# Second spline layer: eight slices in sixteen as rounded halves, and another order of the work between the two spline layers

## The chip, the cores and the metric

The kernel runs on one core of one Trainium2 chip. The metric is the device time of one execution in microseconds; lower is better. The profiled execution gives the trace that all rows are from.

## The reference, cut to what matters

A batch of 32 images and texts becomes 164 tokens each of width 192 (5248 rows in all), which pass attention and then a network of two spline layers with a residual. The change lies in the second of these layers.

```
def bspline_basis(x, num_cp=16, degree=3, rmin=-4.0, rmax=4.0):   # (N, D) -> (N, D, 16)
    ...
def kan_layer(x, w):                       # w: (Dout, Din, num_cp)
    return jnp.einsum('ndk,odk->no', bspline_basis(x), w)
...
# h: (5248, 192); w1: (512, 192, 16); w2: (192, 512, 16); n: the layer norm
y = h + kan_layer(kan_layer(layernorm(h), w1), w2)
```

So layer 2 is a product of 5248 rows with 512 x 16 = 8192 terms each by an 8192 x 192 matrix, all in float32.

## The kernel before

The program is written by hand: each engine has its queue of instructions in a fixed order, and semaphores tie them together. `wait_ge(s, n)` holds an engine's queue until s has reached n. The spline phase (`spline_phase`, from L1507) comes after attention and ends the kernel.

**Layer 1** works on 16 tiles (`PAIRS`) of 328 tokens. Per tile VectorE forms masks times basis values (`take1`, L1715) into a ring of four buffers `spline1_f`, and TensorE multiplies them in eight halves j by the weights, which are stored as a rounded high part and a rounded rest (`w_high`, `w_low`, three matmuls each, L1949 to L1951). TensorE counts a half as done on `f_used`. ScalarE empties the four sums of a tile into `hid` (`empty`, L1879), and SyncE stores them to `hid_scr` (`leave`, L1592, counted on `hid_out`).

**Layer 2** works on 41 tiles (`OT`) of 128 tokens. A tile q has four groups i = 0 to 3, a group sixteen slices r of 128 terms. The first `SETS` = 7 slices of a group go as rounded halves: the high half of the values against both halves of the weights in one matmul of 384 columns (L1977), and the low half of the values against the high half of the weights (192 columns, L1978). The other nine are full float32 matmuls (L1981), which the trace shows as two records each. Group 0 uses the values themselves (`v_high`, `v_low`, `b_`), groups 1 to 3 the values times a mask, which VectorE forms with three instructions each (`take2`, L1726: high, low, rest, of `SPLIT` = 896, 896 and 1152 elements). Before that the values of a tile need:

- on ScalarE `before2` (L1846): positions (four activations, L1842), three folds (L778, L780, L782), the outer square (L786); then `after2` (L1854): rounding to the interval number n (L775) and the inner square (L789, L791); and `high2` (L1864), the rounded high half of the values
- on VectorE `outer` (L799), `inner` (L803), `minus_value` (L1732), and `low2` (L1703), the low half
- at the end of a tile VectorE adds the residual from the sum (`leave`, L1794, L1797), and SyncE stores it.

`tile2` (L1765 on VectorE, L1917 on ScalarE) sets the order: VectorE prepares tile q + 1 between the masks of tile q.

**Between the layers** lies the change. The weights of layer 2 take the place of those of layer 1: raw weights are loaded into room that layer 1's halves leave (`RAW_FREE`, `REST_FREE`), ScalarE rounds them to the high half in four parts (`weight2_high(i)`, L1869, when `f_used` reaches `HIGH_FREE[i]`), and VectorE forms the low half (`weight2_low(i)`, L1762). TensorE waits in tile 0 ahead of each group for `w2_in[i]`, for `w2_ready` at i + 1, and for its masks. ScalarE's order between the layers, by hand:

```
high2(0, 0)
weight2_high(0)
weight2_high(1)
act.wait_ge(f_ready, L1F * PAIRS)
before2(0, 1, 1)
after2(1, 1)
weight2_high(2)
before2(1, 2, 0)
empty(PAIRS - 1)
weight2_high(3)
high2(1, 1)
```

`f_ready` at `L1F * PAIRS` says that VectorE has formed all of layer 1's masks. `share` (L103) lays several groups of buffers over the same room.

Of the kernel before, what the change touches and what calls it, by code (L numbers as in the profile page):

```python
# [19 lines left out]
F32 = mybir.dt.float32  # L20
F32R = mybir.dt.float32r
# [4 lines left out]
P = 128  # L26
# [17 lines left out]
PAIRS = B // 2  # L44
PT = 2 * TOK
# [1461 lines left out]
def spline_phase(nc, front, a, h_scr, hid_scr, step_scr, out, w_raw, w1_in):  # L1507
# [9 lines left out]
    MC = HID // P  # L1517
# [6 lines left out]
    C2_ = 4 * HID  # L1524
    SETS = 7
    SPLIT = SETS * P
# [3 lines left out]
    with ExitStack() as stack:  # L1530
        sb, ps, sem = memories(nc, stack)
        layer1_weights = [(f"spline1_weights_{k}", [P, HALVES, HALF * HID], F32R) for k in ("low", "high")]
        raw_weights = [("spline2_under", [P, HALVES * HALF * HID], F32), ("spline2_weights_raw", [P, 4, SETS * D], F32)]
        layer2_room = [(f"spline2_v_{k}{u}", [P, SPLIT], F32R) for k in ("high", "low") for u in range(2)] + [
            ("spline2_s", [P, C2_], F32), ("spline2_f_low1", [P, SPLIT], F32R),
            ("spline2_gap", [P, HIGH_AT - 5 * SPLIT - C2_], F32),
            ("spline2_weights_split", [P, 2, 4, SETS * D], F32R), ("spline2_weights", [P, 4, 4 * CH - SETS, D], F32)]
        (w_low, w_high), (_, w2_raw), spare = share(nc, stack, layer1_weights, raw_weights, layer2_room)
        v_high, v_low, s_ = [y[:] for y in spare[0:2]], [y[:] for y in spare[2:4]], spare[4][:]
        w2_split, w2 = spare[7:9]  # L1540
        f, f2 = share(nc, stack, [(f"spline1_f{i}", [P, C2_], F32R) for i in range(RING)],
                      [(f"spline2_f_high{i}", [P, SPLIT], F32R) if n == 0 else
                       (f"spline2_f{i}", [P, C2_ - SPLIT], F32) for i in range(1, 4) for n in range(2)] +
                      [(f"spline2_f_low{i}", [P, SPLIT], F32R) for i in range(2, 4)] +
                      [("spline2_f_gap", [P, C2_ - 2 * SPLIT], F32)])
        f_high, f_rest = (None, *f2[0:6:2]), (None, *f2[1:6:2])
        f_low = (None, spare[5], *f2[6:8])
        step_to, step_from = sb("spline2_step_to", [P, PART]), sb("spline2_step_from", [P, PART])
        n_, t_, a_, b_ = ([of, sb(f"spline_{k}1", [P, C2_])] for k, of in
                          (("n", front.n), ("t", front.t), ("a", front.a), ("b", front.b)))  # L1550
        bias2, x, xn = front.bias2, front.x, front.xn
        hid = [sb(f"spline1_hid{m}", [P, PT]) for m in range(MC)]
        acc = ps("spline1_acc", [P, MC, 512])
# [141 lines left out]
        def _(dve):  # L1695
# [69 lines left out]
            def tile2(tt, u, first=False, more=True, early=False):  # L1765

                q, v = 2 * tt + u, 1 - u
                if first:
                    weight2_low(0)
                    weight2_low(1)  # L1770
                take2(q, u, 1)
                if more:
                    front.outer(nc, dve, PAIRS + q + 1, a_[v][:], t_[v][:])
                if first:
                    weight2_low(2)
                take2(q, u, 2)
                if more:
                    front.inner(nc, dve, PAIRS + q + 1, b_[v][:], t_[v][:])
                    minus_value(q + 1, v)
                if first:  # L1780
                    weight2_low(3)
                take2(q, u, 3)
                if more:
                    low2(q + 1, v)
                if not first:
                    leave(tt - 1 if u == 0 else tt, q - 1, v, early)
# [31 lines left out]
        def _(act):  # L1818
# [85 lines left out]
            act.wait_ge(f_used, S_FREE)  # L1904
            high2(0, 0)
            weight2_high(0)
            weight2_high(1)
            act.wait_ge(f_ready, L1F * PAIRS)
            before2(0, 1, 1)
            after2(1, 1)  # L1910
            weight2_high(2)
            before2(1, 2, 0)
            empty(PAIRS - 1)
            weight2_high(3)
            high2(1, 1)
# [232 lines left out]
```

## Time and profile before

| | before |
|---|---|
| median of 3 runs | 2387.16 us (2383.34 to 2398.32) |
| the profiled execution | 2391.56 us, its span 2389.8 us |
| mean granted TensorE clock | 0.978 of 2.4 GHz |
| TensorE matmuls busy | 2277.9 us (95%) |
| VectorE busy | 1846.9 us (77%) |
| ScalarE busy | 1411.4 us (59%) |

The span runs from the first to the last instruction; the time of the execution lies 1.8 us above it. Layer 1 runs from about 857 to 1558.5 us of the span, layer 2 from there to 2386.9. All start times are microseconds from the start of the span. In the rows PE is TensorE's matmuls, PEld its weight loads, DVE VectorE, ACT ScalarE, POOL GpSimd.

### The profile page before, as it was taken

What the parts mean: (1) busy time and instruction counts of PE and PEld (TensorE: products, weight loads), DVE (VectorE), ACT (ScalarE), POOL (GpSimd) and SP (SyncE); (2) the same over time, 40 slices, a digit from 0 to 9 for tenths busy, and PEclk for the clock granted to TensorE, in tenths of its full rate; (3) what the DMA queues carried; (4) which work ended last, traced back from release to release, by engine and by line L of the source; (5) the groups of instructions that cost most, each with busy time, mean ns of one, the idle gap of its engine ahead of it and who ended that gap; (6) DMA issues with size and microseconds to landing.
All of it is one profiled execution on the core that took longest, in us unless ns stands there. A gap on an engine that the chain in (4) does not pass through costs nothing.

```text
span 2389.8 us, 49107 instructions
## 1 busy us (share of the span) xinstructions
PE 2277.9 (95%) x20033; PEld 2134.9 (89%) x20033; DVE 1846.9 (77%) x2241; ACT 1411.4 (59%) x1391; POOL 302.1 (13%) x169
## 2 busy tenths in 40 slices
PE   6599989999999989999999999979999999999999
PEld 5366777888888789999999999979999999999999
DVE  7699756666666587776767766579999999999995
ACT  6488303444444554435435345399888888888881
POOL 7622000000000021322322321000000000000000
PEclk9799998999999889999999999989999999999999
DMA  6655241111111101111111110210000000000000
GB/s 206 179 155 149 67 153 28 51 47 48 48 47 48 36 26 47 42 46 53 46 50 45 49 52 24 88 62 24 23 23 23 23 23 23 23 23 23 23 19 10
DMA packets 115454, 129.98 MB, mean 54 GB/s; under 512 B 17063, under 2 KB 106167, under 8 KB 115127
## 3 DMA queue, kind: packets, MB, share of 16 engines
q1 hardware_dynamic: 95215, 103.54, 14.5%
q10 hardware_dynamic: 16520, 14.34, 2.0%
q0 software_dynamic: 3616, 10.54, 1.7%
q8 instruction: 87, 1.43, 0.2%
q14 instruction: 16, 0.13, 0.0%
HBM read 92.79 MB, written 35.58 MB: 54 GB/s over the span
## 4 chain that ended last, share of the span: by engine, by line
PE 62%; ACT 1%; DVE 0%; issue 0%; ACTq 0%
PE spline_acc L1981 20%; PE spline_acc L1950 10%; PE spline_acc L1949 10%; PE spline_acc L1951 9%; PE spline_acc L1977 9%; PE spline_acc L1978 4%; PE spline_xT L764 0%; ACT spline_s L1842 0%; ACT spline_weights_split L1869 0%; DVE spline_f L1715 0%; ACT spline_t L778 0%; ACT spline_t L780 0%; ACT spline_front L778 0%; ACT spline_front L780 0%; ACT spline_t L782 0%
## 5 line engine op out<-in xcount | busy, mean ns | idle before, releaser
L1950 PE MATMUL spline_acc<-spline_f,spline_weights_high 128*128 128x328 f32 x1536 | 483.3, 315 | 0.0
L1949 PE MATMUL spline_acc<-spline_f,spline_weights_high 128*128 128x328 f32 x1536 | 480.6, 313 | 2.5 <-DVE spline_weights_low L1698 2.5
L1951 PE MATMUL spline_acc<-spline_f,spline_weights_low 128*128 128x328 f32 x1536 | 477.1, 311 | 0.0
L1981 PE MATMUL spline_acc<-spline_weights,spline_f 128*128 128x192 f32 x2214 | 382.7, 327 | 0.0
L1981 PEld LDWEIGHTS spline_acc<-spline_weights,spline_f 128*128 128x128 f32 x2214 | 356.8, 190 | 0.0
L1949 PEld LDWEIGHTS spline_acc<-spline_f,spline_weights_high 128*128 128x128 f32 x1536 | 290.7, 189 | 2.8 <-DVE spline_weights_low L1698 2.8
L1950 PEld LDWEIGHTS spline_acc<-spline_f,spline_weights_high 128*128 128x128 f32 x1536 | 289.6, 189 | 0.0
L1951 PEld LDWEIGHTS spline_acc<-spline_f,spline_weights_low 128*128 128x128 f32 x1536 | 289.3, 188 | 0.0
L1977 PE MATMUL spline_acc<-spline_weights_split,spline_f_high 128*128 128x384 f32 x861 | 274.0, 382 | 14.8 <-DVE spline_f L1726 14.8
L1715 DVE SCALAR_TENSOR_TENSOR spline_f<-spline_front 128x984 fp32r<-128x984 f32 x128 | 148.0, 1196 | 93.6 <-PE spline_acc L1951 88.3
L1978 PE MATMUL spline_acc<-spline_weights_split,spline_f_low 128*128 128x192 f32 x861 | 217.8, 253 | 0.0
L1977 PEld LDWEIGHTS spline_acc<-spline_weights_split,spline_f_high 128*128 128x128 f32 x861 | 163.8, 190 | 15.3 <-issue 15.3
L1021 DVE TENSOR_REDUCE attend_max<-scores_by_query 82x6 f32<-82x876 f32 x128 | 135.4, 1058 | 44.9 <-PE scores_by_query L1352 43.0
L1879 ACT ACTIVATE spline_hid<-spline_acc 128x328 f32<-128x328 f32 x64 | 28.1, 444 | 235.6 <-PE spline_acc L1951 235.6
L1978 PEld LDWEIGHTS spline_acc<-spline_weights_split,spline_f_low 128*128 128x128 f32 x861 | 166.5, 193 | 0.0
L1194 ACT ACTIVATE attend_probs<-scores_by_key 82x1752 f32<-82x1752 f32 x64 | 104.3, 1630 | 90.1 <-PE scores_by_key L1374 90.1
L1715 DVE SCALAR_TENSOR_TENSOR spline_f<-spline_n,spline_a 128x984 fp32r<-128x984 f32 x64 | 77.5, 1210 | 92.4 <-PE spline_acc L1951 91.6
L574 ACT ACTIVATE spline_front<-spline_front,pixel_neg 120x576 f32<-120x576 f32 x160 | 109.7, 763 | 13.3 <-DMA spline_front<-pos_scr 12.0
L551 DVE TENSOR_TENSOR hat_weights<-spline_front,spline_weights_raw 120x2880 f32<-120x2880 f32 x32 | 101.1, 3158 | 3.3 <-PE sample_acc L604 1.0
L745 POOL COPY spline_xn<-spline_xn 82x256 f32<-82x256 f32 x16 | 94.2, 5886 | 72.7 <-DVE spline_xn L686 72.7
L604 PE MATMUL sample_acc<-hat_weights,spline_x 120*96 120x288 f32 (+1 forms) x320 | 84.1, 419 | 19.5 <-DVE hat_weights L551 18.4
L1842 ACT ACTIVATE spline_s<-spline_xn,spline_offset 128x512 f32<-128x512 f32 x160 | 101.8, 707 | 0.0
(240 smaller groups left out, 4894.4 us busy)
## 6 DMA issues: line engine op xcount, KB each, us to landing
spline_front<-pos_scr SPq DMA_DIRECT2D x32, 540.0 KB, 4.4
hid_scr<-spline_hid SPq DMA_DIRECT2D x64, 164.0 KB, 1.8
spline_xn<-hid_scr SPq DMA_DIRECT2D x41, 256.0 KB, 3.1
attend_spread<-rec_scr SPq DMA_DIRECT2D x128, 61.5 KB, 2.2
pix_scr<-spline_front SPq DMA_DIRECT2D x32, 225.0 KB, 3.3
spline_weights_raw<-w SPq DMA_DIRECT2D x1, 6144.0 KB, 21.4
spline_step_to<-w SPq DMA_DIRECT2D x36, 128.0 KB, 2.1
spline_step_from<-w SPq DMA_DIRECT2D x36, 128.0 KB, 2.1
```

Source lines behind the costliest of these rows:

```text
L551: nc.vector.tensor_tensor(wt[0:PIXC, u], dy[u][0:PIXC], hx[u][0:PIXC, :].rearrange("p (a n) -> p a n", a=1) .to_broadcast([PIXC, NPIXC, SA ...
L574: nc.scalar.activation(dy[u][0:PIXC, part, :].rearrange("p (k n) -> p k n", k=TAPS), p[:, 0], ACT.Abs, bias=neg[0:PIXC, part:part + 1])
L1021: nc.vector.tensor_reduce(mx[0:ROWS, n, 2 * h:2 * h + 2, 0:HG], sc[0:ROWS, :, 0:SW].rearrange("p j (g n) -> p j g n", n=SPAN), AX_X, ALU.m ...
L1194: nc.scalar.activation(prT[0:ROWS, c, :, FROM[c]:FROM[c] + SPAN].rearrange("p (j g) n -> p j g n", j=4), tp[0:ROWS, :, 0:SW].rearrange("p ...
L1715: nc.vector.scalar_tensor_tensor(f[j % RING][:, part * HC:(part + 1) * HC], n_[u][:, cols], MAGIC + i, v[:, cols], ALU.is_equal, ALU.mult) ...
L1842: nc.scalar.activation(dst[:, r * HID:(r + 1) * HID].rearrange("p (c n) -> p c n", c=CH), x2[u], ACT.Identity, bias=bias2[:, r:r + 1], sca ...
L1949: nc.tensor.matmul(z, high, x_high, start=start, stop=False)
L1950: nc.tensor.matmul(z, high, x_low, start=False, stop=False)
L1951: last = nc.tensor.matmul(z, low, x_high, start=False, stop=stop)
L1977: nc.tensor.matmul(acc2[:, u, 0:2 * D], high[:, cols], both, start=start, stop=False)
L1978: last = nc.tensor.matmul(z, low[:, cols], both[:, 0], start=False, stop=False)
L1981: last = nc.tensor.matmul(z, rest[:, cols], w2[:, i, r - SETS, :], start=False, stop=stop)
```

## The change

`SETS` goes from 7 to 8, so eight of sixteen slices are rounded halves, and `SPLIT` from 896 to 1024. The rounded masks (`f_high`, `f_low`), `v_high`, `v_low` and the rounded weights grow, and the parts in full float32 shrink: by 128 elements per partition in a mask, by 192 in a quarter of the weights. The second `v_low` no longer has room beside the weights and lies over `hid`, layer 1's output buffers; so VectorE waits for `hid_out` at `16 * PAIRS` (the last tile of layer 1 is stored) before `low2` of tile 1. The gaps in the layout close up, and by this `HIGH_FREE` becomes 125, 126, 127, 128 (it was 126, 127, 128, 128); `RAW_FREE` (121 to 124) and `REST_FREE` (125 to 128) stay.

On ScalarE `before2` of tile 1 moves ahead of the first two roundings, the roundings 2 and 3 stand together behind `after2` of tile 1, and the last `empty` and `before2` of tile 2 change places. On VectorE, for tile 0 alone, `outer` of tile 1 moves between the low halves 0 and 1, and `inner` and `minus_value` of tile 1 behind the last masks, so that the three `take2` of tile 0 come one after the other with only the low halves 2 and 3 between them.

```diff
-    SETS = 7
+    SETS = 8
...
-        layer2_room = [(f"spline2_v_{k}{u}", [P, SPLIT], F32R) for k in ("high", "low") for u in range(2)] + [
+        layer2_room = [(f"spline2_v_{k}{u}", [P, SPLIT], F32R) for k, u in (("high", 0), ("high", 1), ("low", 0))] + [
...
-            ("spline2_gap", [P, HIGH_AT - 5 * SPLIT - C2_], F32),
...
+        hid, (v_low1, _) = share(nc, stack, [(f"spline1_hid{m}", [P, PT], F32) for m in range(MC)],
+                                 [("spline2_v_low1", [P, SPLIT], F32R),
+                                  ("spline2_hid_rest", [P, MC * PT - SPLIT], F32)])
...
                 if first:
                     weight2_low(0)
+                    front.outer(nc, dve, PAIRS + q + 1, a_[v][:], t_[v][:])
                     weight2_low(1)
                 take2(q, u, 1)
-                if more:
+                if more and not first:
                     front.outer(nc, dve, PAIRS + q + 1, a_[v][:], t_[v][:])
                 if first:
                     weight2_low(2)
                 take2(q, u, 2)
-                if more:
+                if more and not first:
                     front.inner(nc, dve, PAIRS + q + 1, b_[v][:], t_[v][:])
                     minus_value(q + 1, v)
                 if first:
                     weight2_low(3)
                 take2(q, u, 3)
+                if first:
+                    front.inner(nc, dve, PAIRS + q + 1, b_[v][:], t_[v][:])
+                    minus_value(q + 1, v)
+                if first:
+                    for m in range(MC):
+                        dve.wait_ge(hid_out[m], 16 * PAIRS)
                 if more:
                     low2(q + 1, v)
...
             high2(0, 0)
+            act.wait_ge(f_ready, L1F * PAIRS)
+            before2(0, 1, 1)
             weight2_high(0)
             weight2_high(1)
-            act.wait_ge(f_ready, L1F * PAIRS)
-            before2(0, 1, 1)
             after2(1, 1)
             weight2_high(2)
+            weight2_high(3)
+            empty(PAIRS - 1)
             before2(1, 2, 0)
-            empty(PAIRS - 1)
-            weight2_high(3)
             high2(1, 1)
```

## Rows read from the trace of the kernel before

**Rows 1.** The page's busy times of the engines: us (share of the span) and instructions.
```profile
PE 2277.9 (95%) x20033; PEld 2134.9 (89%) x20033; DVE 1846.9 (77%) x2241; ACT 1411.4 (59%) x1391; POOL 302.1 (13%) x169
```

**Rows 2.** Windows. Each: its length, busy time of each engine, TensorE's granted clock, DMA share.
```profile
334.30:336.60 2.30, 0.05 (x2) 0.07 (x2) 1.89 (x8) 0.00 (x0) 0.10 (x1) 1.00 0.97 329
...
338.00:341.50 3.50, 3.50 (x15) 3.50 (x13) 0.90 (x3) 0.62 (x2) 0.00 (x0) 0.51 0.98 421
...
1568.50:1573.50 5.00, 0.05 (x1) 0.00 (x0) 1.45 (x1) 4.97 (x6) 0.00 (x0) 1.00 0.00 0
...
1577.00:1580.40 3.40, 3.37 (x13) 3.40 (x14) 3.30 (x2) 3.37 (x2) 0.00 (x0) 0.50 0.00 0
...
1583.50:1587.20 3.70, 0.29 (x2) 0.00 (x0) 2.11 (x2) 2.40 (x4) 0.00 (x0) 1.00 0.75 246
...
1616.50:2386.80 770.30, 770.30 (x4995) 770.18 (x4993) 695.89 (x576) 625.27 (x441) 0.00 (x0) 1.00 0.08 22
```

**Rows 3.** Waits: who waited for whom: total us, times, longest. Above 1530:1610, below 1610:2390.
```profile
PE spline_acc L1977 <- DVE spline_f L1726: 14.8, 2, 8.5
...
DVE spline_f_high L1726 <- PE spline_acc L1981: 53.6, 39, 1.6
```

**Rows 4.** Timeline of TensorE, second layer: start, us, what; [idle before].
```profile
1596.82 0.47 PE L1977 MATMUL spline_acc<-spline_weights_split,spline_v_high 128*128 128x384 f32 x1
...
1598.38 0.36 PE L1977 MATMUL spline_acc<-spline_weights_split,spline_v_high 128*128 128x384 f32 x1
1598.58 0.25 PE L1978 MATMUL spline_acc<-spline_weights_split,spline_v_low 128*128 128x192 f32 x1
1598.67 0.37 PE L1977 MATMUL spline_acc<-spline_weights_split,spline_v_high 128*128 128x384 f32 x1
...
1598.96 3.11 PE L1981 MATMUL spline_acc<-spline_weights,spline_b 128*128 128x192 f32 x18
...
2381.72 0.47 PE L1977 MATMUL spline_acc<-spline_weights_split,spline_f_high 128*128 128x384 f32 x1
```

**Rows 5.** Timeline of VectorE around the handover.
```profile
1539.71 1.18 DVE L1715 SCALAR_TENSOR_TENSOR spline_f<-spline_n,spline_t 128x984 fp32r<-128x984 f32 x1
...
1558.76 1.09 DVE L1726 SCALAR_TENSOR_TENSOR spline_f_high<-spline_front,spline_v_high 128x896 fp32r<-128x896 f32 x1 [2.41 <-PE spline_acc L1951]
...
1572.06 1.56 DVE L1762 TENSOR_TENSOR spline_weights_split<-spline_weights_raw,spline_weights_split 128x1344 fp32r<-128x1344 f32 x1 [4.46 <-ACT spline_weights_split L1869]
1573.53 1.08 DVE L1726 SCALAR_TENSOR_TENSOR spline_f_high<-spline_front,spline_v_high 128x896 fp32r<-128x896 f32 x1
...
1594.12 2.29 DVE L799 SCALAR_TENSOR_TENSOR spline_front<-spline_front 128x2048 f32<-128x2048 f32 x1
1596.32 1.08 DVE L1726 SCALAR_TENSOR_TENSOR spline_f_high<-spline_n,spline_v_high 128x896 fp32r<-128x896 f32 x1
...
1598.32 1.35 DVE L1726 SCALAR_TENSOR_TENSOR spline_f<-spline_n,spline_b 128x1152 f32<-128x1152 f32 x1
1599.59 2.29 DVE L803 SCALAR_TENSOR_TENSOR spline_front<-spline_front 128x2048 f32<-128x2048 f32 x1
...
1604.19 1.08 DVE L1726 SCALAR_TENSOR_TENSOR spline_f_high<-spline_n,spline_v_high 128x896 fp32r<-128x896 f32 x1
```

**Rows 6.** Timeline of ScalarE around the handover.
```profile
1538.79 0.96 ACT L1864 ACTIVATE spline_v_high<-spline_front 128x896 fp32r<-128x896 f32 x1 [6.60 <-DVE spline_front L1732]
...
1553.43 1.33 ACT L1869 ACTIVATE spline_weights_split<-spline_weights_raw 128x1344 fp32r<-128x1344 f32 x1 [4.06 <-PE spline_acc L1951]
1554.66 2.54 ACT L1842 ACTIVATE spline_s<-spline_xn,spline_offset 128x512 f32<-128x512 f32 x4
...
1565.17 1.90 ACT L775 ACTIVATE spline_n<-spline_s 128x2048 f32<-128x2048 f32 x1
...
1570.72 1.31 ACT L1869 ACTIVATE spline_weights_split<-spline_weights_raw 128x1344 fp32r<-128x1344 f32 x1
...
1583.72 1.34 ACT L1869 ACTIVATE spline_weights_split<-spline_weights_raw 128x1344 fp32r<-128x1344 f32 x1
```

More of the change, by code:

```diff
@@ L1533, in spline_phase @@
         raw_weights = [("spline2_under", [P, HALVES * HALF * HID], F32), ("spline2_weights_raw", [P, 4, SETS * D], F32)]
-        layer2_room = [(f"spline2_v_{k}{u}", [P, SPLIT], F32R) for k in ("high", "low") for u in range(2)] + [
+        layer2_room = [(f"spline2_v_{k}{u}", [P, SPLIT], F32R) for k, u in (("high", 0), ("high", 1), ("low", 0))] + [
             ("spline2_s", [P, C2_], F32), ("spline2_f_low1", [P, SPLIT], F32R),
-            ("spline2_gap", [P, HIGH_AT - 5 * SPLIT - C2_], F32),
             ("spline2_weights_split", [P, 2, 4, SETS * D], F32R), ("spline2_weights", [P, 4, 4 * CH - SETS, D], F32)]
         (w_low, w_high), (_, w2_raw), spare = share(nc, stack, layer1_weights, raw_weights, layer2_room)
-        v_high, v_low, s_ = [y[:] for y in spare[0:2]], [y[:] for y in spare[2:4]], spare[4][:]
-        w2_split, w2 = spare[7:9]
+        hid, (v_low1, _) = share(nc, stack, [(f"spline1_hid{m}", [P, PT], F32) for m in range(MC)],
+                                 [("spline2_v_low1", [P, SPLIT], F32R),
+                                  ("spline2_hid_rest", [P, MC * PT - SPLIT], F32)])
+        v_high, v_low, s_ = [y[:] for y in spare[0:2]], [spare[2][:], v_low1[:]], spare[3][:]
+        w2_split, w2 = spare[5:7]
         f, f2 = share(nc, stack, [(f"spline1_f{i}", [P, C2_], F32R) for i in range(RING)],
@@ L1543, in spline_phase @@
                        (f"spline2_f{i}", [P, C2_ - SPLIT], F32) for i in range(1, 4) for n in range(2)] +
-                      [(f"spline2_f_low{i}", [P, SPLIT], F32R) for i in range(2, 4)] +
-                      [("spline2_f_gap", [P, C2_ - 2 * SPLIT], F32)])
+                      [(f"spline2_f_low{i}", [P, SPLIT], F32R) for i in range(2, 4)])
         f_high, f_rest = (None, *f2[0:6:2]), (None, *f2[1:6:2])
-        f_low = (None, spare[5], *f2[6:8])
+        f_low = (None, spare[4], *f2[6:8])
         step_to, step_from = sb("spline2_step_to", [P, PART]), sb("spline2_step_from", [P, PART])
@@ L1551, in spline_phase @@
         bias2, x, xn = front.bias2, front.x, front.xn
-        hid = [sb(f"spline1_hid{m}", [P, PT]) for m in range(MC)]
         acc = ps("spline1_acc", [P, MC, 512])
```

## The prediction

> **What bounds the kernel now.** I read the page first, then windows, then each engine's timeline around the change. TensorE is busy 2278 of 2390 us, the other engines far less [rows 1]. The windows show two different stretches [rows 2]. From 1616.5 us to the end TensorE is busy all of the time at a granted clock of 1.00, so the second layer is bound by TensorE alone: VectorE works 695.9 of 770.3 us there and ScalarE 625.3. Before that, at the handover between the layers, TensorE stops twice. The first stop begins at 1568.55, behind group 1 of tile 0, the second at 1583.8, behind group 2; they last 8.5 and 6.3 us, 14.8 together [rows 3]. After the first the clock is 0.50 (1.2 GHz) for 3.4 us [rows 2]. So the change must be read at two places: the pace of a slice in the long stretch, and which engine is last at the handover.
>
> A tile q of the second layer has four groups (i = 0 to 3) of sixteen slices. Group starts lie 4.936 us apart: (2381.72 - 1596.82) / 159 [rows 4]. Tile 0 began at 1558.5, right behind layer 1. Four groups without a stop would be 19.7 us, thus tile 1 would start at 1578.3; it starts at 1596.82. So 18.5 us are lost at the handover: 14.8 us of stops, and the other 3.7 are about what two stretches at half clock lose.
>
> Who was last? VectorE forms the weights' low halves (L1762) in the same queue as the masks, each behind a rounding on ScalarE (L1869). At 1572.06 VectorE had waited 4.46 us for the third rounding [rows 5], which ScalarE began only at 1570.72, behind ten microseconds of tile 1's folds and five of its inner square [rows 6]. The fourth waited behind the folds of tile 2 and the four emptyings, until 1583.72 [rows 6]. These two waits are the two stops.
>
> **Part 1, slices.** One slice of sixteen goes from full fp32 to halves. A split slice costs 0.29 us in the group shown (0.20 from 1598.38 to 1598.58, 0.09 to 1598.67), as a mean over the start times of all 160 such groups 0.200 + 0.088 = 0.288. A full slice is two records: (3.11 - 0.326) / 17 = 0.164 us each, and without the first of the eighteen, which comes a little late, 0.1625, so 0.325 us per slice [rows 4]. The first slice of a group costs 0.11 us more in both kernels. Saved: 0.037 us per group, so a group takes 4.899 and a tile 19.60 us. Bounds: 0.033 (0.325 against 0.292, the slowest split slices) and 0.040 (0.328, two records of 0.164, against 0.288); over 160 groups that is 5.3 to 6.4 us.
>
> A rule that would give more: by the Trainium skill, FP8 and Floating Point Precision, section TensorE Precision Notes, true FP32 makes four passes through the array. By columns alone four passes of 192 against the three that the halves need would save a quarter of 0.325, 0.08 us a slice or 13 us in all (rival 2). The measured 0.288 doesn't agree: halves cost more than their columns, so the row decides.
>
> **Part 2, VectorE's price.** A mask costs 1.05 ns more per element: (1.35 - 1.08) / 256 [rows 5]. The two rounded masks grow by 128 elements each, the rest shrinks by 128: a take2 of three goes from 3.27 (1596.32 to 1599.59) to 3.41 us. With three of them and the low half of the values that is 0.54 us more per tile. VectorE idles for TensorE 53.6 us over 39 tiles, 1.37 us a tile [rows 3]; 0.54 more work and a tile shorter by 0.15 leave 0.68 us. It stays hidden. If that cover were gone, every further 0.1 us would cost 4 us. ScalarE's high half grows by 0.11 us (0.82 ns per element: 1.90 for 2048, 0.96 for 896 [rows 6]) against 3.7 us of idle time a tile (145.0 over 39 [rows 2]); hidden as well.
>
> **Part 3, the handover.** The chain follows from the order of the queues. ScalarE: high2 of tile 0 starts at 1538.79 and lasts 0.96 + 0.11. The wait for all of layer 1's masks is over at 1540.9 (the last one starts at 1539.71 and takes 1.18 [rows 5]), while TensorE has 17.6 us of layer 1 in stock. So before2 of tile 1, which costs 10.5 us (1554.66 to 1565.17 [rows 6]), runs from 1540.9 to 1551.4, thirteen microseconds earlier. Then two roundings of 1.38 us (1.23 from 1553.43 to the next start, plus 192 elements): ends 1552.9 and 1554.2. Room for each of the four is free at 1542.2, 1547.7, 1553.1 and 1558.6, since TensorE releases a half of tile 15 every 5.4 us (rounding two of before was released near 1553.3 [rows 6], the masks by the last half near 1558.6 [rows 5]); so none of them waits. after2 (5.55 us, 1565.17 to 1570.72) to 1559.8, roundings three and four to 1561.2 and 1562.5, the emptyings to 1563.8 (they move ahead of before2 of tile 2, and their four stores on SyncE's queue with them; behind those stand the loads of tile 3's input and the output stores, wanted 20 us later), before2 of tile 2 to 1574.3.
>
> VectorE: low half 0 at 1553.0 (1.47, from 1572.06 to 1573.53, becomes 1.67 us), outer of tile 1 (2.20: 1594.12 to 1596.32) and low half 1 end at 1558.6; the masks can start at 1558.76 as today, when TensorE has left layer 1. Cover here is only 0.2 us: a ScalarE that is later by more moves everything behind it. From there VectorE is the path, without a stop: three take2 (10.23), low halves 2 and 3 (3.34), inner and minus_value together (4.60: 1599.59 to 1604.19 [rows 5]), end 1576.93. Then ScalarE's high2 with its hand-overs (1.3) and low2: TensorE may start tile 1 at 1579.5. The new wait on hid_out stands ahead of low2; the stores are done ten microseconds before, and what is queued behind it (low2, then tile 1's masks) loses nothing. Bounds of that wait: 0, and 0.2 us for four checks if they weren't beside the wait for high2.
>
> TensorE on tile 0: four groups of 4.90 from 1558.56. Group 2 is due at 1568.4 and its masks are there at 1567.3; group 3 is due at 1573.3, masks at 1572.4. Both former stops are gone. It ends at 1578.2 and waits 1.3 us. Tile 1: VectorE works from 1579.43: take2 (3.41), outer (2.20), take2, inner and minus_value (4.60), take2, end 1596.5. Group 3 of tile 1 would be due at 1579.5 + 14.7 = 1594.2, so a second stop of 2.3 us. It starts at 1596.6, against 1611.64 today (1596.82 + 3 x 4.94): 15.0 us gained. Tile 2: VectorE is through with its last masks after another 18.8 us, at 1615.3; TensorE comes to them at 1596.6 + 4 x 4.90 = 1616.2. From there VectorE gains 0.78 us on TensorE with every tile, and no more stops come.
>
> **The clock.** In the first stop it was still at 1.00 in the 5.0 us from 1568.5 on, and in the second through 3.7 us from 1583.5. Against that, after 2.3 us at 334.3 in which TensorE did almost nothing, and 1.4 us of work, there came 3.5 us at 0.51 [rows 2]. So a stop of 2.3 us may cost a stretch at 1.2 GHz: 3.4 us at half pace lose 1.7 us. Bounds for the two stops: 0 and 3.4 us. I take 0.8, half a stretch, for the longer one, which is about as long as the one at 334.3.
>
> **Sum.** 15.0 (handover) + 157 groups x 0.037 = 5.8 - 0.8 (clock) = 20.0 us. The profiled execution took 2391.6 us (span 2389.8), 4.4 over the median of 2387.2; it becomes 2371.6, and the median 2367.2. That is 0.84%. About 1% (23.9 us) is what a measurement of this kernel can tell from no change; the three runs differ by 15 us.
>
> **Rivals.**
> 1. ScalarE is late (12 in 100). For: the cover at 1558.6 is 0.2 us, that of rounding three 0.9 us. If before2 of tile 1 starts at 1547 instead of 1540.9, behind something that the trace doesn't show, VectorE's row begins 6 us late: 2373. Against: ScalarE began the same step at 1554.66 without a wait, and its room is free by 1538.8, since high2 of tile 0 waits for the same halves.
> 2. Halves at the pace of their columns (8 in 100): a split slice 0.163 + 0.088 = 0.25 us, since two passes of 192 columns take 0.163 in the full slices. Saved then 0.075 x 157 = 11.8 us: 2361. Against: 0.20 in every split slice of the trace but a group's first, which is slower still. By the passes of the Trainium skill, FP8 and Floating Point Precision, this would be the outcome.
> 3. The roundings move, but not the stops (5 in 100): TensorE waits at groups 2 and 3 of tile 0 for weights or masks as before. Only the slices are left, 2381. Against: [rows 5, 6] name the two roundings, and both move ahead.
> 4. VectorE becomes the bound of the second layer (5 in 100), the case on the slow side. At 18.8 us it is 0.78 below TensorE's 19.60. Should wider rounded masks, reads of v_low in its new place or the longer ring with ScalarE (17.2 us per tile: 10.5 + 5.55 + 1.07) add 0.78 us, it sets the pace; the change is slower than before from 19.75 + 15.0 / 39 = 20.13 us a tile, 1.3 us more than my sum. At 20.8 it is 26 us, 2413. Against: the masks' times follow their widths.
>
> **Chances.** The forecast as summed has 70 in 100, with 2360 to 2374 as its own range (clock 0 to 3.4 us, slices 5.3 to 6.4, the run-to-run difference of medians of some 4). To hold 8 in 10 the range takes in rival 2 and most of 1: 2357 to 2378. Faster by over 1% (under 2363.3): the lower fifth of the forecast and most of rival 2, 0.23. Slower by over 1%: part of rival 4, 0.03. Within: 0.74.
>
> **What would show it.** Right: ScalarE's folds of tile 1 start near 1541, ahead of all four roundings; low halves 0 and 1 are done before 1558.7; TensorE runs through tile 0 and stops once for 1.3 us ahead of tile 1 and once for 2.3 us ahead of its group 3; no stop over 3 us; groups 4.90 us apart; VectorE idles some 0.7 us a tile. Wrong: a first stop longer than 3 us, stops that recur after tile 2, groups at 4.94 or 4.86, or VectorE with no idle time in the second layer.

## The result and the profile after

The changed kernel took 2377.01 us as the median of 7 runs, the kernel before 2394.59 us in 7 runs; the ratio is 0.9924 with a 95% interval of 0.9903 to 0.9945, which is 18 us less (13 to 23). The profiled execution of it took 2377.01 us, its span 2375.3. Three executions of the kernels below that took far longer (2543.55, 12438.03 and 6651.43 us) are left out of the ratios as slow ones.

The span is only 14.5 us shorter than before, but the two executions reached the second layer at different times. I take the start of the layer's first matmul and the end of its last from the trace:

| | first matmul | last ends | layer 2 |
|---|---|---|---|
| before | 1558.6 | 2387.0 | 828.4 us |
| changed | 1566.6 | 2372.5 | 805.9 us |

So the layer gained 22.6 us, and 8.0 us were lost ahead of it in this execution. The first fence has lines of the page of the changed kernel. In the last of them ScalarE waited 20.9 us ahead of a step of the first phases, 19.6 of them for a load from `pos_scr`; before it was 13.3 and 12.0 on the same line, which the change doesn't touch. That step began 5.9 us later (96.6 against 90.7 us), layer 1 7.1 us later (864.6 against 857.5), and layer 1 itself took 0.9 us more. The wait's length alone doesn't tell the delay: in a kernel below (`minus_value` late) it was 19.2 us, yet the step began at 92.9, and that trace reached the second layer earliest of all.

```profile
PE 2272.5 (96%) x20033; PEld 2123.1 (89%) x20033; DVE 1870.8 (79%) x2241; ACT 1412.7 (59%) x1391; POOL 297.8 (13%) x169
...
L1984 PE MATMUL spline_acc<-spline_weights_split,spline_f_high 128*128 128x384 f32 x984 | 304.9, 374 | 2.1 <-DVE spline_f L1726 2.1
...
L574 ACT ACTIVATE spline_front<-spline_front,pixel_neg 120x576 f32<-120x576 f32 x160 | 109.7, 763 | 20.9 <-DMA spline_front<-pos_scr 19.6
```

Over all thirteen executions that were profiled in this study the second layer begins between 1556.5 and 1568.5 us, in no order with the kernels. A change of 20 us is hard to weigh by whole times with that. The step just named begins between 87.2 and 99.2 us, so most of that range is there ahead of attention already. Two traces of the changed kernel differ in the layer's own time by 1.6 us, by one cause, shown below. From its first matmul to that of layer 2, layer 1 takes 700.9 to 702.5 us in all of them.

TensorE's waits at the handover, which answer to [rows 3], and VectorE's for TensorE over the layer:

```profile
PE spline_acc L1984 <- DVE spline_f L1726: 2.1, 1, 2.1
PE spline_acc L1984 <- DVE spline_v_low L1703: 1.2, 1, 1.2
...
DVE spline_f_high L1726 <- PE spline_acc L1988: 21.7, 31, 1.4
```

Two stops of 2.1 and 1.2 us stand where 14.8 us were. VectorE idles 0.70 us a tile (21.7 over 31) where it waits for TensorE (it was 1.37, in 39 tiles); in the first tiles behind the handover it waits for nothing, since it is still behind. The timeline of ScalarE of the changed kernel, against [rows 6]; the layer begins at 1566.6, so 8.0 is to be taken off for a comparison:

```profile
1546.75 1.06 ACT L1871 ACTIVATE spline_v_high<-spline_front 128x1024 fp32r<-128x1024 f32 x1 [6.66 <-DVE spline_front L1732]
1548.87 2.56 ACT L1849 ACTIVATE spline_s<-spline_xn,spline_offset 128x512 f32<-128x512 f32 x4 [1.06 <-DVE spline_f L1715]
...
1559.40 2.85 ACT L1876 ACTIVATE spline_weights_split<-spline_weights_raw 128x1536 fp32r<-128x1536 f32 x2
...
1567.71 2.84 ACT L1876 ACTIVATE spline_weights_split<-spline_weights_raw 128x1536 fp32r<-128x1536 f32 x2
1570.45 1.42 ACT L1886 ACTIVATE spline_hid<-spline_acc 128x328 f32<-128x328 f32 x4
1572.14 2.56 ACT L1849 ACTIVATE spline_s<-spline_xn,spline_offset 128x512 f32<-128x512 f32 x4 [0.27 <-DMA spline_xn<-hid_scr]
```

The step for tile 1 starts 17.7 us ahead of the layer, and four roundings run in two pairs without a wait for room. VectorE's timeline, against [rows 5]:

```profile
1560.90 1.76 DVE L1762 TENSOR_TENSOR spline_weights_split<-spline_weights_raw,spline_weights_split 128x1536 fp32r<-128x1536 f32 x1 [10.93 <-ACT spline_weights_split L1876]
...
1564.78 1.75 DVE L1762 TENSOR_TENSOR spline_weights_split<-spline_weights_raw,spline_weights_split 128x1536 fp32r<-128x1536 f32 x1
1566.77 1.23 DVE L1726 SCALAR_TENSOR_TENSOR spline_f_high<-spline_front,spline_v_high 128x1024 fp32r<-128x1024 f32 x1 [0.24 <-PE spline_acc L1958]
...
1580.33 2.29 DVE L803 SCALAR_TENSOR_TENSOR spline_b<-spline_t,spline_b 128x2048 f32<-128x2048 f32 x1
1582.73 2.29 DVE L1732 SCALAR_TENSOR_TENSOR spline_b<-spline_a,spline_b 128x2048 f32<-128x2048 f32 x1
1586.24 1.23 DVE L1703 TENSOR_TENSOR spline_v_low<-spline_b,spline_v_high 128x1024 fp32r<-128x1024 f32 x1 [1.22 <-ACT spline_v_high L1871]
...
1603.27 1.22 DVE L1726 SCALAR_TENSOR_TENSOR spline_f<-spline_n,spline_b 128x1024 f32<-128x1024 f32 x1
```

VectorE waits 0.24 us for the end of layer 1, then works without a gap to 1585.0, waits 1.2 us for `high2`, and works on to the last masks of tile 1 at 1604.5. TensorE starts that group at 1604.54. The distances of the group starts (first split matmul to first split matmul) are 4.74, 4.89, 4.89, 6.42, 4.85, 4.89, 7.28, and from there 4.889 us on average; before they were 4.78, 13.69, 13.04, 6.75, and then 4.9365.

### The profile page after: what moved, and what is told of

Same layout as the page of the kernel before. It is cut to its first block, busy times and chain, and to the rows that moved or that the text cites. A ratio compares the mean times of both kernels' runs of the same rounds, so it can differ in the third digit from the quotient of the medians.

```text
span 2375.3 us, 49109 instructions
## 1 busy us (share of the span) xinstructions
PE 2272.5 (96%) x20033; PEld 2123.1 (89%) x20033; DVE 1870.8 (79%) x2241; ACT 1412.7 (59%) x1391; POOL 297.8 (13%) x169
## 3 DMA queue, kind: packets, MB, share of 16 engines
q1 hardware_dynamic: 95215, 103.54, 14.5%
## 4 chain that ended last, share of the span: by engine, by line
PE 62%; DVE 2%; ACT 0%; issue 0%; DVEq 0%
PE spline_acc L1988 17%; PE spline_acc L1984 10%; PE spline_acc L1956 10%; PE spline_acc L1958 10%; PE spline_acc L1957 10%; PE spline_acc L1985 5%; PE spline_xT L764 0%; DVE spline_f L1726 0%; DVE spline_f_high L1726 0%; DVE spline_f_low L1726 0%; DVE spline_weights_split L1762 0%; DVE spline_b L1732 0%; DVE spline_front L1732 0%; DVE spline_f L1715 0%; DVE spline_front L803 0%; DVE spline_b L803 0%
## 5 line engine op out<-in xcount | busy, mean ns | idle before, releaser
L1988 PE MATMUL spline_acc<-spline_weights,spline_f 128*128 128x192 f32 x1968 | 342.5, 327 | 0.0
L1988 PEld LDWEIGHTS spline_acc<-spline_weights,spline_f 128*128 128x128 f32 x1968 | 316.6, 190 | 0.0
L1984 PE MATMUL spline_acc<-spline_weights_split,spline_f_high 128*128 128x384 f32 x984 | 304.9, 374 | 2.1 <-DVE spline_f L1726 2.1
L1985 PE MATMUL spline_acc<-spline_weights_split,spline_f_low 128*128 128x192 f32 x984 | 248.5, 253 | 0.0
L1985 PEld LDWEIGHTS spline_acc<-spline_weights_split,spline_f_low 128*128 128x128 f32 x984 | 187.9, 191 | 0.0
L1984 PEld LDWEIGHTS spline_acc<-spline_weights_split,spline_f_high 128*128 128x128 f32 x984 | 185.0, 188 | 2.4 <-DVE spline_f L1726 2.4
L1715 DVE SCALAR_TENSOR_TENSOR spline_f<-spline_n,spline_a 128x984 fp32r<-128x984 f32 x64 | 77.5, 1211 | 91.6 <-PE spline_acc L1958 90.7
L574 ACT ACTIVATE spline_front<-spline_front,pixel_neg 120x576 f32<-120x576 f32 x160 | 109.7, 763 | 20.9 <-DMA spline_front<-pos_scr 19.6
L604 PE MATMUL sample_acc<-hat_weights,spline_x 120*96 120x288 f32 (+1 forms) x320 | 84.1, 419 | 19.2 <-DVE hat_weights L551 17.5
```

The lines of the kernel that those rows point to most:

```text
L574: nc.scalar.activation(dy[u][0:PIXC, part, :].rearrange("p (k n) -> p k n", k=TAPS), p[:, 0], ACT.Abs, bias=neg[0:PIXC, part:part + 1])
L1715: nc.vector.scalar_tensor_tensor(f[j % RING][:, part * HC:(part + 1) * HC], n_[u][:, cols], MAGIC + i, v[:, cols], ALU.is_equal, ALU.mult) ...
L1984: nc.tensor.matmul(acc2[:, u, 0:2 * D], high[:, cols], both, start=start, stop=False)
L1985: last = nc.tensor.matmul(z, low[:, cols], both[:, 0], start=False, stop=False)
L1988: last = nc.tensor.matmul(z, rest[:, cols], w2[:, i, r - SETS, :], start=False, stop=stop)
```

## The experiments

Most verdicts are read from the second layer's own time, first matmul to last, as in the table above. For each kernel the waits are TensorE's at the handover: total us, times, longest. The ratio stands beside them, against runs of the kernel before on the same chip. Each layer time is from a single trace; the changed kernel traced twice gave 805.9 and 807.4 us, so a difference of 1.6 us needs a reason that the trace shows. "Half clock" is TensorE at 1.2 GHz, a granted clock near 0.50 in a window.

**Order alone.** Seven rounded slices and the old layout, both queues in the new order (without the wait on `hid_out`).

```diff
 # the kernel before, with
-            weight2_high(0)
-            weight2_high(1)
             act.wait_ge(f_ready, L1F * PAIRS)
             before2(0, 1, 1)
+            weight2_high(0)
+            weight2_high(1)
             after2(1, 1)
             weight2_high(2)
+            weight2_high(3)
+            empty(PAIRS - 1)
             before2(1, 2, 0)
-            empty(PAIRS - 1)
-            weight2_high(3)
 # and VectorE's tile 0 as in the change
```

> Seven rounded slices as before, both new orders. I compare the second layer from its first matmul to its last: 828.4 us before, 805.9 after the change. Theory (VectorE's chain sets the handover, slices are a separate term): VectorE's chain is shorter than in the changed kernel (masks 3.27, low halves 1.47 us), so a stop of about 0.1 us ahead of tile 1 and 1.7 us ahead of its group 3, which starts 36.4 us into the layer; with 157 groups of 4.9365 us the layer takes 811.7 us, 16.7 less than before, ratio about 0.993. Rival (the gain needs the eighth rounded slice, since with it the room for the roundings comes one half earlier): the roundings of 126, 127, 128, 128 come later, the stops stay above 3 us and the layer takes over 815 us.

Measured: layer 811.7 us, as computed; ratio 0.9915 (0.9883 to 0.9947).

```profile
PE spline_acc L1981 <- DVE spline_f L1726: 1.6, 1, 1.6
```

One stop of 1.6 us where 1.7 was computed; the 0.1 us computed ahead of tile 1 is no stop in the trace. The order alone brings 16.7 of the 22.6 us. With the shorter masks of seven slices the handover is even 1.5 us better than in the changed kernel; the slices return more than that, 7.4 us.

**Slices alone.** `SETS` = 8 and the new layout, both queues in the old order.

```diff
 # the changed kernel, with both orders of the kernel before; on VectorE:
                 take2(q, u, 3)
+                if first:
+                    for m in range(MC):
+                        dve.wait_ge(hid_out[m], 16 * PAIRS)
                 if more:
                     low2(q + 1, v)
```

> Eight rounded slices and the new layout, both orders as before. Theory: groups of 4.889 us instead of 4.9365; room for the first two roundings comes one half (5.4 us) earlier, so ScalarE's step for tile 1 starts near 9.5 us ahead of the layer; stops of 3.5 us ahead of group 2 and 8.4 us ahead of group 3, a stretch at half clock after the longer one; the layer takes about 815.4 us, 13.0 less than before, of which 7.5 are slices. Rival (the layout brings nothing to the handover): stops as before, 14.8 us together, layer 820 to 821 us.

Measured: layer 815.9 us; ratio 0.9921 (0.9891 to 0.9950).

```profile
PE spline_acc L1980 <- DVE spline_f L1726: 8.8, 2, 5.0
```

The two stops sum to 8.8 us where I had expected 11.9: they were 3.8 (3.5 computed) and 5.0 (8.4 computed). But each was followed by half clock: group 2 took 3.0 and group 3 1.5 us more than 4.89. Three microseconds that I had put into the second stop were half clock behind the first, so the layer's time came out (815.4 computed) with its parts wrong. The layout does help the handover: of the 12.5 us gained, 7.4 are slices, and 5 come from room for the roundings being free one half of layer 1 earlier: ScalarE's step for tile 1 began 9.1 us ahead of the layer, where it was 3.9. So slices and order aren't two separate parts: 12.5 and 16.7 don't add up to 22.6.

**ScalarE's order alone** (the change, VectorE's tile 0 in the old order).

```diff
                 if first:
                     weight2_low(0)
-                    front.outer(nc, dve, PAIRS + q + 1, a_[v][:], t_[v][:])
                     weight2_low(1)
                 take2(q, u, 1)
-                if more and not first:
+                if more:
                     front.outer(nc, dve, PAIRS + q + 1, a_[v][:], t_[v][:])
...
-                if more and not first:
+                if more:
                     front.inner(nc, dve, PAIRS + q + 1, b_[v][:], t_[v][:])
                     minus_value(q + 1, v)
...
                 take2(q, u, 3)
-                if first:
-                    front.inner(nc, dve, PAIRS + q + 1, b_[v][:], t_[v][:])
-                    minus_value(q + 1, v)
```

> The change with VectorE's order of tile 0 left as before (inner and minus_value of tile 1 ahead of the fourth low half). Theory: VectorE's chain decides, so its order matters: stops of 1.3 us ahead of group 2 and 4.8 us ahead of group 3, none ahead of tile 1; layer 807.8 us, or 809.5 if the clock falls after the longer stop. Rival (ScalarE's order is the whole gain): layer 805.9 us or less, as in the changed kernel.

Measured: layer 811.1 us; ratio 0.9909 (0.9874 to 0.9943).

```profile
PE spline_acc L1980 <- DVE spline_f L1726: 5.7, 2, 4.5
```

Stops of 1.2 and 4.5 us, as computed (1.3 and 4.8), yet the layer took 1.6 us more than the upper figure. Windows of this kernel, from within the longer stop on, show why (length; busy times; then the granted clock, third from the end):

```profile
1584.80:1588.00 3.20, 0.00 (x0) 0.00 (x0) 3.20 (x4) 0.68 (x1) 0.00 (x0) 1.00 0.00 0
1588.00:1592.00 4.00, 2.74 (x10) 2.77 (x11) 4.00 (x4) 2.85 (x2) 0.00 (x0) 0.57 0.00 0
1592.00:1596.00 4.00, 4.00 (x18) 4.00 (x17) 4.00 (x4) 3.97 (x5) 0.00 (x0) 0.58 0.00 0
1596.00:1600.00 4.00, 4.00 (x28) 4.00 (x27) 4.00 (x4) 3.94 (x5) 0.00 (x0) 1.00 0.02 4
```

The clock fell late in the stop and stayed down for most of the eight microseconds of the two middle windows, in which TensorE worked 6.7; group 3 took 7.70 us, 2.8 more than 4.89. I had priced a stretch at 1.7. So VectorE's order is worth 5.2 us beside ScalarE's.

**VectorE's order alone** (the change, ScalarE in the old order).

```diff
             high2(0, 0)
-            act.wait_ge(f_ready, L1F * PAIRS)
-            before2(0, 1, 1)
             weight2_high(0)
             weight2_high(1)
+            act.wait_ge(f_ready, L1F * PAIRS)
+            before2(0, 1, 1)
             after2(1, 1)
             weight2_high(2)
-            weight2_high(3)
-            empty(PAIRS - 1)
             before2(1, 2, 0)
+            empty(PAIRS - 1)
+            weight2_high(3)
```

> The change with ScalarE's order left as before. Theory: the fourth rounding is again behind the folds of tile 2; outer of tile 1 holds up the second low half: stops of 3.7 us ahead of group 1 and 8.1 us ahead of group 3, layer about 818 us, worse than the split alone (815.4). Rival (VectorE's row of masks is the gain): layer at 808 us or less.

Measured: layer 818.8 us; ratio 0.9939 (0.9910 to 0.9968).

```profile
PE spline_acc L1984 <- DVE spline_f L1726: 10.4, 3, 4.9
```

Stops of 3.7 and 8.1 us were computed; they are 4.0 ahead of group 1, 4.9 ahead of group 3, and 1.6 ahead of group 3 of tile 1, and the groups behind the first two took 3.0 and 2.5 us more at half clock. As with the slices alone, the layer's time came out (818 computed) with its parts wrong. It is 2.9 us worse than no change of order at all (815.9): `outer` of tile 1 stands ahead of the second low half, and with ScalarE's old order its input isn't there (VectorE waits 14.2 us for it). VectorE's order has its worth only with ScalarE's; ScalarE's alone brought 4.9 us (811.1 against 815.9), and both together 10.1.

**The change again.**

> The changed kernel once more, in the same hour and on the same chip as the next kernels. Theory: second layer 805.9 us again, stops of 1.2 and 2.1 us at a clock of 1.00, groups of 4.889 us; what differs from execution to execution lies ahead of the second layer. Rival (the slices or the stops vary): layer off by more than 0.5 us.

Measured: 2370.69 us, ratio 0.9925 (0.9902 to 0.9948); layer 807.4 us. The stops were the same (2.0 and 1.2 us), the groups 4.889, but the group behind the longer stop took 1.6 us more. Its windows, from that stop on:

```profile
1595.50:1597.60 2.10, 0.40 (x3) 0.40 (x4) 2.10 (x3) 0.71 (x2) 0.00 (x0) 1.00 0.00 0
1597.60:1599.00 1.40, 1.40 (x10) 1.40 (x9) 1.37 (x4) 1.40 (x1) 0.00 (x0) 0.74 0.00 0
1599.00:1602.50 3.50, 3.50 (x16) 3.50 (x15) 3.50 (x4) 3.47 (x3) 0.00 (x0) 0.61 0.33 95
1602.50:1606.00 3.50, 3.50 (x26) 3.50 (x25) 3.50 (x3) 3.39 (x6) 0.00 (x0) 1.00 0.14 41
```

And the same stretch of the changed kernel's first trace:

```profile
1602.60:1604.70 2.10, 0.16 (x1) 0.16 (x2) 2.10 (x3) 0.71 (x2) 0.00 (x0) 1.00 0.00 0
1604.70:1606.00 1.30, 1.30 (x10) 1.30 (x11) 1.26 (x3) 1.30 (x1) 0.00 (x0) 1.00 0.00 0
1606.00:1609.50 3.50, 3.50 (x25) 3.50 (x23) 3.50 (x4) 3.47 (x3) 0.00 (x0) 1.00 0.26 74
```

The same stop of 2 us led to half clock in one execution and not in the other; why, isn't shown. My theory had 805.9 us and a clock of 1.00, so the rival was right in its letter: the layer varies, by this.

**VectorE's cover.** The change, and from tile 4 on four VectorE instructions per tile with 1024 elements in all, whose results nobody reads.

```diff
                 for u in range(2):
                     tile2(tt, u)
+                    for more_out in (step_to, step_from, hid_rest, extra):
+                        w = more_out.shape[-1]
+                        some = w2[:, 0].rearrange("p r o -> p (r o)")[:, 0:w]
+                        nc.vector.scalar_tensor_tensor(more_out[:], some, 0.0, some, ALU.min, ALU.subtract)
```

> The change, plus four VectorE instructions of 1024 elements in all per tile, from tile 4 on, that nobody needs: 1.35 us more work a tile. Theory (VectorE has 0.7 us a tile of cover): it becomes the bound at 20.15 us a tile against 19.56, so after a head start of some 2.4 us the layer grows by about 0.6 x 37 - 2.4 = 20 us, to 826 us, and VectorE no longer waits for TensorE. Rival (the masks run far enough ahead, or ScalarE's ring is the tighter one): growth under 5 us, or over 30.

Measured: layer 824.6 us, with the 1.6 us of half clock behind the stop of 2.1, so 17.1 more than the kernel just above. Waits from 1640 us on; VectorE no longer waits for TensorE, and TensorE, matmuls and weight loads, waits for masks:

```profile
PEld spline_acc L1989 <- DVE spline_f L1727: 17.5, 29, 0.6
PE spline_acc L1989 <- DVE spline_f L1727: 8.9, 28, 0.3
```

With 1.35 us more a tile, VectorE is the bound. From tile 12 on TensorE takes 20.15 us a tile, as computed; it is 17 us and not the 20 computed because TensorE kept its own 19.56 us up to tile 10, so the head start was larger than the 2.4 us that I had put.

**GpSimd for two low halves.** The stops that are left come from VectorE's chain, and GpSimd has nothing to do there.

```diff
+            for i in (2, 3):                      # on GpSimd, behind its last step
+                pool.wait_ge(w2_high_ready, i + 1)
+                pool.wait_ge(w2_ready, i)
+                pool.tensor_tensor(w2_split[:, 1, i], w2_raw[:, i], w2_split[:, 0, i].bitcast(F32),
+                                   ALU.subtract).then_inc(w2_ready, 1)
...
-                if first:                         # on VectorE
-                    weight2_low(2)
...
-                if first:
-                    weight2_low(3)
```

> The change with the low halves 2 and 3 of the weights formed on GpSimd, which is idle then, instead of VectorE. Theory (VectorE's chain sets what is left of the handover): its chain is 3.3 us shorter. No stop ahead of tile 1; the stop ahead of its group 3 shrinks only to about 1.3 us, because ScalarE is then the late one (high2 of tile 1 stands behind before2 of tile 2, which ends 16.2 us into the layer). GpSimd needs some 5 us each and is through 8 and 13 us into the layer, before groups 2 and 3 at 9.6 and 14.5. Layer about 803.9 us, 2 less than the changed kernel. Rival (another thing holds the two stops, or GpSimd slows VectorE down): 805.9 us or more.

Measured: layer 809.2 us, 3.3 worse than the changed kernel's 805.9; ratio 0.9905 (0.9878 to 0.9933). Whole times don't show that: their medians are 2367.39 us here and 2370.69 for the changed kernel on the same chip. The verdict rests on the trace. The timeline of this kernel, VectorE and then GpSimd:

```profile
1562.80 1.22 DVE L1731 SCALAR_TENSOR_TENSOR spline_f<-spline_front 128x1024 f32<-128x1024 f32 x1
1563.93 4.51 DVE L1731 SCALAR_TENSOR_TENSOR spline_f_high<-spline_front,spline_v_high 128x1024 fp32r<-128x1024 f32 x1
1568.37 4.48 DVE L1731 SCALAR_TENSOR_TENSOR spline_f_low<-spline_front,spline_v_low 128x1024 fp32r<-128x1024 f32 x1
1572.77 1.21 DVE L1731 SCALAR_TENSOR_TENSOR spline_f<-spline_front 128x1024 f32<-128x1024 f32 x1
...
1563.02 8.74 POOL L1696 TENSOR_TENSOR spline_weights_split<-spline_weights_raw,spline_weights_split 128x1536 fp32r<-128x1536 f32 x2 [111.01 <-ACT spline_weights_split L1877]
```

Two masks that take 1.22 us took 4.5 us each while GpSimd's two subtractions ran (8.7 us, 4.3 each), and the mask behind them 1.21 again. So VectorE lost 6.6 us to be relieved of 3.3. TensorE stopped 3.9 us ahead of group 2, and that group took 3.0 us more at half clock; the two stops of the changed kernel were gone. By the Trainium skill, SBUF — State Buffer, section Who interferes with whom, a VectorE instruction with two SBUF inputs contends with a GpSimd instruction that reads SBUF, and the ports that the two share are an exclusive lock. The 4.5 us agree: each mask ended about 1.1 us behind the end of a subtraction, as if it had waited for that and then run.

**The same with ScalarE's `high2` of tile 1 ahead of the outer square of tile 2.**

```diff
-            before2(1, 2, 0)
+            act.wait_ge(n_ready, PAIRS + 2)
+            position(1, 2, 0, s_)
+            act.wait_ge(v_ready, PAIRS + 1)
+            front.folds(nc, act, PAIRS + 2, s_, t_[0][:])
             high2(1, 1)
+            front.square_outer(nc, act, PAIRS + 2, a_[0][:], t_[0][:])
```

> As the kernel with GpSimd's low halves, and ScalarE's high2 of tile 1 ahead of the outer square of tile 2. Theory: ScalarE is no longer late, high2 runs at 15.1 us into the layer, the last stop shrinks to 0.2 us: layer about 802.8 us, 3.1 less than the changed kernel, 25.6 less than before. Rival (the square of tile 2 comes too late for VectorE): 803.9 us or more.

Measured: layer 809.1 us, where 802.8 were expected; ratio 0.9923 (0.9897 to 0.9949): two masks took 4.5 us again, the stop ahead of group 2 was 3.9 again, and behind it there was nothing for the edit to gain.

**`minus_value` late.** If VectorE's chain is the bound, what stands ahead of the masks without need is worth moving.

```diff
                 take2(q, u, 2)
                 if more and not first:
                     front.inner(nc, dve, PAIRS + q + 1, b_[v][:], t_[v][:])
-                    minus_value(q + 1, v)
                 if first:
                     weight2_low(3)
                 take2(q, u, 3)
                 if first:
                     front.inner(nc, dve, PAIRS + q + 1, b_[v][:], t_[v][:])
+                if more:
                     minus_value(q + 1, v)
                 if first:
                     for m in range(MC):
                         dve.wait_ge(hid_out[m], 16 * PAIRS)
-                if more:
-                    low2(q + 1, v)
                 if not first:
                     leave(tt - 1 if u == 0 else tt, q - 1, v, early)
+                if more:
+                    low2(q + 1, v)
```

> The change, and in every tile VectorE does minus_value of the next tile behind the third masks instead of ahead of them, and the residual ahead of low2, where it fills the wait for ScalarE's high2. Theory (the stop ahead of group 3 of tile 1 is minus_value standing ahead of the masks): the stop of 1.2 us ahead of tile 1 stays, the one of 2.1 us goes, and VectorE needs 19.4 us a tile against TensorE's 19.56, so no other stop comes: layer 803.8 us, and no half-clock stretch. Rival (the waiting for high2 in every tile makes VectorE the bound): groups over 4.89 us on average and a layer over 806 us.

Measured: layer 803.5 us; 2371.73 us, ratio 0.9899 (0.9874 to 0.9925). TensorE's only stop, and VectorE's waits over the layer:

```profile
PE spline_acc L1984 <- DVE spline_v_low L1703: 1.2, 1, 1.2
...
DVE spline_v_low L1703 <- ACT spline_v_high L1871: 19.3, 40, 1.2
...
DVE spline_f_high L1726 <- PE spline_acc L1988: 7.1, 17, 1.4
```

VectorE now waits some 0.5 us a tile for `high2`, and for TensorE only 7.1 us in all: the reserve is nearly used up, but no group comes late. The layer took 803.5 us where 803.8 were computed.

**Both: `minus_value` late as above, and ScalarE's roundings between its steps.**

```diff
             act.wait_ge(f_ready, L1F * PAIRS)
-            before2(0, 1, 1)
+            act.wait_ge(n_ready, PAIRS + 1)
+            position(0, 1, 1, s_)
             weight2_high(0)
+            front.folds(nc, act, PAIRS + 1, s_, t_[1][:])
             weight2_high(1)
-            after2(1, 1)
+            front.square_outer(nc, act, PAIRS + 1, a_[1][:], t_[1][:])
             weight2_high(2)
+            after2(1, 1)
             weight2_high(3)
...
                     weight2_low(0)                # VectorE, ahead of tile 0's masks
-                    front.outer(nc, dve, PAIRS + q + 1, a_[v][:], t_[v][:])
                     weight2_low(1)
+                    front.outer(nc, dve, PAIRS + q + 1, a_[v][:], t_[v][:])
+                    weight2_low(2)
...
-                if first:                         # behind the first masks
-                    weight2_low(2)
```

> As the kernel with minus_value late, and ScalarE's first three roundings between the steps of tile 1 (each when its room is just free), so that VectorE forms the low halves 0 to 2 in the 10.9 us that it idles ahead of the layer. Theory: VectorE's chain in tile 0 is 1.7 us shorter, the stop ahead of tile 1 goes too: layer 802 us, TensorE without a stop from layer 1 to the end. Rival (a rounding waits for its room and makes ScalarE late): a stop in tile 0 or ahead of tile 1, layer over 803.5 us.

Measured: layer 802.0 us, 26.4 less than before; 2372.94 us, ratio 0.9895 (0.9862 to 0.9928). The window over the whole layer:

```profile
1562.70:2364.70 802.00, 801.95 (x5249) 801.65 (x5247) 758.38 (x610) 668.07 (x476) 0.00 (x0) 1.00 0.08 24
```

TensorE has no stop left, as computed. This is the best version of the layer; by whole times it can't be told from the one before it, nor with certainty from the changed kernel, whose interval overlaps.

**Six slices.** The change with `SETS` = 6, gaps put back into the layout.

```diff
-    SETS = 8
+    SETS = 6
...
+            ("spline2_gap", [P, HIGH_AT - 4 * SPLIT - C2_], F32),
```

> The change's orders with six rounded slices. Theory (a rounded slice saves the same each time, 0.047 us a group, and it is TensorE's pace alone): groups of 4.984 us, no stop ahead of tile 1, one of 0.3 us ahead of its group 3, layer 817.5 us. Rival (the last slice saved more than the ones before, since eight and eight records end in step): groups of 4.974 us (0.037 a slice), layer 816.

Measured (one execution): groups of 4.968 us, layer 815.4. So 4.968, 4.9365, 4.889 for six, seven and eight: the seventh slice saved 0.032 us a group and the eighth 0.047. Neither theory had it: the saving isn't the same each time, and the average, 0.040, is nearer to the rival's.

## Why the prediction came out right, and where not

**Handover: right.** 15.0 us were computed; from the layer's first matmul to group 3 of tile 1 it is 53.1 us before and 38.0 after, so 15.1. The stops were to be 1.3 and 2.3 us and are 1.2 and 2.1; the cover ahead of the first masks was to be 0.2 and is 0.24. The reason holds up when its parts are undone: the same arithmetic gave 811.7 for the order alone (811.7), 803.8 for `minus_value` late (803.5) and 802 for the version without stops (802.0). That VectorE's queue is the path at the handover is shown by these last two: taking `minus_value` out of its way removes the stop ahead of group 3, and moving a low half ahead of the layer removes the one ahead of tile 1. The useless work of 1.35 us a tile shows something else, namely how much VectorE has to spare in the long stretch. Where a stop of 3.8 us or more came first, the arithmetic missed the stop behind it, by 3.4 us (slices alone) and 3.2 (VectorE's order alone), above all since it left out half clock.

**Slices: the term was too small.** 157 x 0.037 = 5.8 us were forecast, 157 x 0.047 = 7.4 measured, outside my bounds of 5.3 to 6.4 by 1 us. I exchanged one slice at the prices of the layer before and took the other fifteen as fixed. Of the 0.047, some 0.010 come from the seven split slices that were there already: the distance from their first matmul to the second went from 0.200 to 0.198. Why the slice's price moves with their number (0.047 for the eighth, 0.032 for the seventh) wasn't tried and stays open.

**Clock: half right.** The forecast took 0.8, half a stretch, for a stop of two microseconds. Of three executions with that same stop, one lost nothing and two lost 1.6 us; 0.8 is a mean that no execution shows. For longer stops the price of 1.7 was wrong: behind stops of 3.8 to 4.9 us the next group took 2.5 to 3.0 us more, against 1.5 and 1.8 behind the two longer ones of before. Windows of the kernel before show why:

```profile
1573.50:1577.00 3.50, 0.00 (x0) 0.00 (x0) 3.50 (x5) 3.44 (x4) 0.00 (x0) 0.52 0.00 0
1577.00:1580.40 3.40, 3.37 (x13) 3.40 (x14) 3.30 (x2) 3.37 (x2) 0.00 (x0) 0.50 0.00 0
...
1587.20:1590.00 2.80, 0.00 (x0) 0.00 (x0) 2.80 (x4) 0.04 (x1) 0.00 (x0) 0.52 0.36 103
1590.00:1594.10 4.10, 4.03 (x15) 4.06 (x16) 4.10 (x4) 4.07 (x3) 0.00 (x0) 0.50 0.00 0
```

Part of the half clock passed while TensorE stood still, and what it cost is half of the rest. The stop's length doesn't fix the price either. Behind the stop of 5.0 us (slices alone) the clock fell only when work resumed, and came back after 3.4 us, so that group took 1.5 us more:

```profile
1580.70:1585.60 4.90, 0.00 (x0) 0.01 (x1) 4.90 (x5) 0.61 (x2) 0.00 (x0) 1.00 0.38 111
1585.70:1589.10 3.40, 3.40 (x13) 3.40 (x14) 3.40 (x4) 3.40 (x2) 0.00 (x0) 0.50 0.00 0
1589.20:1592.50 3.30, 3.30 (x23) 3.30 (x22) 3.30 (x3) 3.27 (x5) 0.00 (x0) 1.00 0.02 5
```

**VectorE's price: right.** 0.70 us of idle time in each tile in which it waits for TensorE, 0.68 forecast.

**Sum.** The layer gave 22.6 us (21.0 with the stretch), against 20.0 (with 0.8 for the clock) in the forecast; whole times gave 18 (13 to 23). In each trace 2.8 us of the span lie behind the layer, so what differs between the layer and the whole lies ahead of it; for the executions that weren't traced this isn't shown.

**The time itself: inside the range by 1 us, and partly by luck.** 2367.2 us were forecast and 2377.0 measured. That is outside the 2360 to 2374 that the forecast gave itself, and inside 2357 to 2378 only because the range had been widened for rivals that didn't come true. Of the 9.8 us, 7.4 come from the kernel before, whose median went from 2387.2 us in three executions to 2394.6 in seven; the other 2.4 are the difference between 20.0 and 17.6 saved. The profiled execution (2371.6 forecast, 2377.0 measured) began the layer 8.0 us later and saved 2.6 us more in it. The right part is the mechanism and the saving, not the absolute time.

**Rivals.** ScalarE late: it began the step 1.1 us after `high2` of tile 0, as computed. Halves at the pace of their columns: 0.198 between the two matmuls of a slice, not 0.163. Stops unchanged: they are gone. VectorE as the bound: it has 0.7 us a tile to spare, and the kernel with more work shows what lies beyond.

## What to carry to other kernels

When an engine's queue is the path through a handover, write down its instructions in order with their durations, and do the same for the engine that feeds it; here that gave stops to 0.2 us where no half clock came between, and it told which order to change next. Two orders that depend on each other must be tried together: beside the slices ScalarE's alone brought 4.9 us and VectorE's alone -2.9, both together 10.1. Weigh such a change by the stage's own time in the trace when the stages ahead of it vary by as much as the gain.

## What the runs showed of the hardware

- GpSimd and VectorE, both subtracting or masking with two inputs from SBUF: VectorE's mask took 4.5 us instead of 1.22 while GpSimd worked. Work moved to an idle GpSimd isn't free.
- The same stop of TensorE of 2.0 to 2.1 us was followed by 1.2 GHz in two executions of three, and not in the third. Behind a stop of 4.5 us the granted clock was 0.57 over eight microseconds. A shorter stop can so cost more behind it (2.8 us) than one of 8.5 us (1.5).
- A rounded slice of 384 and 192 columns takes 0.286 to 0.288 us against 0.325 for the full one (two records), and the saving per slice depends on how many there are (0.032, then 0.047).
